# Weighted sums of the last layer: three products of rounded halves in place of one fp32 product, one step later

## What is computed

```python
S = S + jnp.eye(n, dtype=S.dtype)
h = x @ W
scores = h @ U @ h.T
mask = S > 0
scores = jnp.where(mask, scores, -jnp.inf)
att = jax.nn.softmax(scores, axis=-1)
att = att * mask.astype(att.dtype)
S_tilde = S * att
return S_tilde @ h
```

## Time and profile before

| what | us |
|---|---|
| median of three runs | 448.84 |
| the profiled execution | 449.18 |
| its span in the profile | 447.4 |
| TensorE busy (matmuls) | 404.3 |
| VectorE busy | 348.7 |
| ScalarE busy | 227.5 |
| GpSimd busy | 113.6 |

### The profile page before, as it was taken

The page is one execution under the profiler, slowest core; times in us unless marked ns, Lnnn a source line. Parts: engine busy times, 40 slices in busy tenths (PEclk is TensorE's granted clock), DMA queues, the critical chain, the costliest instruction groups (busy, mean ns, idle before and its releaser), DMA issues.

```text
span 447.4 us, 7537 instructions
## 1 busy us (share of the span) xinstructions
PE 404.3 (90%) x2596; PEld 364.4 (81%) x2596; DVE 348.7 (78%) x808; ACT 227.5 (51%) x467; POOL 113.6 (25%) x126
## 2 busy tenths in 40 slices
PE   7899999999897899999898859999599989999895
PEld 6688888999796799998898758898488778978674
DVE  5599899899875579999999956775567778768872
ACT  2243189989873778897696734214123222212230
POOL 1171000001011259431130205632000024424452
PEclk9699999999998999999999989999699999989989
DMA  8990001000000000000000000000000000010010
GB/s 259 385 370 23 1 1 49 1 0 2 0 2 1 1 1 1 3 0 2 1 0 2 1 1 0 1 1 2 1 0 1 1 1 0 0 48 1 0 48 30
DMA packets 10301, 13.96 MB, mean 31 GB/s; under 512 B 645, under 2 KB 7193, under 8 KB 10265
## 3 DMA queue, kind: packets, MB, share of 16 engines
q1 hardware_dynamic: 10264, 13.49, 8.9%
HBM read 12.10 MB, written 1.39 MB: 30 GB/s over the span
## 4 chain that ended last, share of the span: by engine, by line
PE 70%; DVE 19%; issue 7%; ACT 3%; POOL 0%; DVEq 0%; ACTq 0%
PE ps L1619 12%; PE ps L228 10%; PE ps L230 9%; PE ps L229 9%; PE ps L1355 7%; PE ps L1350 6%; PE ps L1351 6%; PE ps L1573 3%; PE ps L1574 3%; DVE s_sb L982 2%; DVE x_stats L739 2%; DVE p_lo L995 2%; PE ps L1252 2%; DVE p_lo L831 1%; DVE m_sb L817 1%
## 5 line engine op out<-in xcount | busy, mean ns | idle before, releaser
L1619 PE MATMUL ps<-v,w_ring 128*128 128x256 f32 (+3 forms) x242 | 59.1, 396 | 4.8 <-DVE x_sb L1208 3.2
L1350 PE MATMUL ps<-v_hi,p_hi 128*128 128x258 f32 (+3 forms) x242 | 63.0, 291 | 0.5 <-DVE s_sb L1036 0.4
L1351 PE MATMUL ps<-v_lo,p_hi 128*128 128x258 f32 (+3 forms) x242 | 61.1, 282 | 0.0
L1619 PEld LDWEIGHTS ps<-v,w_ring 128*128 128x128 f32 (+3 forms) x242 | 46.0, 194 | 13.4 <-issue 3.7
L228 PE MATMUL ps<-mid_hi,big_hi 128*128 128x512 f32 (+2 forms) x132 | 54.0, 409 | 2.6 <-DVE mid_lo L768 1.6
L295 POOL TENSOR_TENSOR mr_all<-mr_all,mhalf 128x4 f32<-128x4 f32 (+1 forms) x12 | 12.5, 1046 | 159.0 <-DVE mr_all L749 159.0
L391 POOL TENSOR_TENSOR total<-total,s_sb 128x512 f32<-128x512 f32 (+3 forms) x27 | 30.8, 1140 | 83.9 <-DVE w_ring L1196 83.9
L229 PE MATMUL ps<-mid_lo,big_hi 128*128 128x512 f32 (+2 forms) x132 | 49.2, 372 | 0.0
L230 PE MATMUL ps<-mid_hi,big_lo 128*128 128x512 f32 (+2 forms) x132 | 49.1, 372 | 0.0
L1350 PEld LDWEIGHTS ps<-v_hi,p_hi 128*128 128x128 f32 (+3 forms) x242 | 44.7, 185 | 2.4 <-issue 1.2
L1351 PEld LDWEIGHTS ps<-v_lo,p_hi 128*128 128x128 f32 (+3 forms) x242 | 44.7, 185 | 0.3
(11 more groups left out here) (180 smaller groups left out, 1079.5 us busy)
## 6 DMA issues: line engine op xcount, KB each, us to landing
adjT_sb<-in_adjT_dram SPq DMA_DIRECT2D x1, 2816.0 KB, 16.6
adjT_sb<-in_adjT_dram SPq DMA_DIRECT2D x3, 768.0 KB, 9.7
adjT_sb<-in_adjT_dram SPq DMA_DIRECT2D x1, 1815.0 KB, 20.9
out_dram<-x_sb SPq DMA_DIRECT2D x10, 128.0 KB
x_sb<-in_x_dram SPq DMA_DIRECT2D x2, 512.0 KB, 4.7
adjT_sb<-in_adjT_dram SPq DMA_DIRECT2D x1, 512.0 KB, 11.4
rows_sb<-in_rows_dram SPq DMA_DIRECT2D x1, 385.0 KB, 11.0
s_sb<-in_wq_dram SPq DMA_DIRECT2D x1, 256.0 KB, 4.3
```

What stands on the lines that cost most here:

```text
L1350: pe.matmul(out_ap, left_[0][0:k, n % RING, mine], right_[0][0:k, j, 0:cols_], start=(j == 0), stop=False)
L1351: pe.matmul(out_ap, left_[0][0:k, n % RING, mine], right_[1][0:k, j, 0:cols_], start=False, stop=False)
L1619: ins = pe.matmul(ps[0:rows(b), B3.sums[b % PER], 0:D], w_ring[0:k, n % RING, mine], v3[0:k, j, :], start=(j == 0), stop=(j == NB - 1))
```

## The change

- The values of the last layer go to `v_hi` as rounded halves (ScalarE), and VectorE makes their rest in the new `values3_lo(b)`, in step b (blocks 9 and 10 in step 10, block 8 in step 9). TensorE's `values(b)` now waits for that of block b - 2.
- `times_s(n)` writes an fp32 tile `full(n)` (two of them). The new `w_hi(n)` on ScalarE, behind `exp3(n + 1)`, rounds it into `p_lo`; the new `weights3_lo(n)` takes the rest into `w_lo`, on VectorE at the end of step n + 15 for even n, on GpSimd behind `add_total(n)` for odd n. `times_s(n)` waits for the rest of tile n - 2, and the copy and the rest wait for the sum of tile n - 3.
- `aggregate3` calls `weighted`: per block hi*hi and hi*lo, then, once the rest is there, lo*hi. It is a step later (LAG3 = 16), `out3` of groups 0 and 1 too (s = 11 gi + 27). `add_up` stays where it was.
- The tiles move: `total` to `raw_a` and `raw_b`, which are idle by then, and the two new weight tiles to the room of `gram`, `w3T_sb` and `u3T_sb`. `v3`, `w_ring` and the old `total` go.

```diff
--- before.py
+++ after.py
@@ -24,6 +24,7 @@
 NT = NG * NB
 CW = [min(BANK, N - g * BANK) for g in range(NG)]
 LAG = 15
+LAG3 = 16
 SLOTS = 15
 SLOTS3 = 18
 RING = 3
@@ -85,13 +86,7 @@
             p_hi, p_lo = sb("p_hi", [P, RING, BANK], F32R, early), sb("p_lo", [P, RING, BANK], F32R, early)
         more = sb("more", [P, 2 * RING, BANK])
 
-        with ExitStack() as early:
-            v_hi, v_lo = sb("v_hi", [P, NB, W], F32R, early), sb("v_lo", [P, NB, W], F32R, early)
-        with ExitStack() as late:
-            v3 = sb("v3", [P, NB, D], F32, late)
-            w_ring = sb("w_ring", [P, RING, BANK], F32, late)
-            total = sb("total", [P, 2, BANK], F32, late)
-        sb("v_home", [P, 2 * NB * W])
+        v_hi, v_lo = sb("v_hi", [P, NB, W], F32R), sb("v_lo", [P, NB, W], F32R)
 
         with ExitStack() as early:
             asa_sb = sb("asa_sb", [P, 2, D], F32, early)
@@ -102,8 +97,11 @@
         wa_hi, wa_lo = sb("wa_hi", [P, C, WA], F32R), sb("wa_lo", [P, C, WA], F32R)
         wb_hi, wb_lo = sb("wb_hi", [P, C, W], F32R), sb("wb_lo", [P, C, W], F32R)
         raw_a, raw_b = sb("raw_a", [P, C, WA]), sb("raw_b", [P, C, W])
-        gram = sb("gram", [P, C, D])
-        w3T_sb, u3T_sb = sb("w3T_sb", [P, C, D]), sb("u3T_sb", [P, C, D])
+        with ExitStack() as early:
+            gram = sb("gram", [P, C, D], F32, early)
+            w3T_sb, u3T_sb = sb("w3T_sb", [P, C, D], F32, early), sb("u3T_sb", [P, C, D], F32, early)
+        w_lo = sb("w_lo", [P, RING, BANK], F32R)
+        w_full = sb("w_full", [P, 2, BANK])
         rows_sb = sb("rows_sb", [P, 3 * D + 2])
         cols_sb = sb("cols_sb", [P, 6, C])
         ident = sb("ident", [P, P])
@@ -140,6 +138,8 @@
         def staged(k):
             return s_sb[:, k, :].rearrange("p (c n) -> p c n", c=C)
 
+        totals = [t[:, :, :].rearrange("p c n -> p (c n)")[:, 0:BANK] for t in (raw_a, raw_b)]
+
         wq_sb, wk_sb = staged(11), staged(12)
         bq_rep = s_sb[:, 14, 0:C * P].rearrange("p (c n) -> p c n", c=C)
         left = s_sb[:, 0:3, :]
@@ -157,6 +157,9 @@
 
         def sum1(n):
             return s_sb[0:rows(n % NB), 9 + n % 6, 0:CW[n // NB]]
+
+        def full(n):
+            return w_full[0:rows(n % NB), n % 2, 0:CW[n // NB]]
 
         def ring(t, n):
             return t[0:rows(n % NB), n % RING, 0:CW[n // NB]]
@@ -216,6 +219,7 @@
         rs_set, rsi_set, sal_set, joined, th_set = (sem(n) for n in ("rs_set", "rsi_set", "sal_set", "joined", "th_set"))
         p2_mm, biased, h2hi, h2lo, mask2, agg2 = (sem(n) for n in ("p2_mm", "biased", "h2hi", "h2lo", "mask2", "agg2"))
         eye_add, w_set, tot_add, tot_mm = sem("eye_add"), sem("w_set"), sem("tot_add"), sem("tot_mm")
+        vlo3, w_hi_set, w_lo_even, w_lo_odd = sem("vlo3"), sem("w_hi_set"), sem("w_lo_even"), sem("w_lo_odd")
 
 
         def wait(eng, s, value):
@@ -387,11 +391,19 @@
                 pool.wait_ge(w_set, n + 1)
                 if j:
                     wait(pool, tot_add, 10 * gi + j - 1)
-                    r = total[0:rows(j), gi % 2, 0:CW[gi]]
+                    r = totals[gi % 2][0:rows(j), 0:CW[gi]]
                     pool.tensor_tensor(r, r, slot3(n), ALU.add).then_inc(tot_add, 1)
+
+            def weights3_lo(n):
+
+                pool.wait_ge(w_hi_set, n + 1)
+                wait(pool, agg[1], n - 2)
+                pool.tensor_tensor(ring(w_lo, n), full(n), f(ring(p_lo, n)), ALU.subtract).then_inc(w_lo_odd, 1)
 
             for n in range(NT):
                 add_total(n)
+                if n % 2:
+                    weights3_lo(n)
 
 
         @block.scalar
@@ -429,8 +441,7 @@
 
                 bank = (B3 if a else B0).values[b % 2]
                 act.wait_ge(v_mm[a], b + 1)
-                dst = v3[0:rows(b), b, :] if a else v_hi[0:rows(b), b, 0:D]
-                act.activation(dst, ps[0:rows(b), bank, 0:D], ACT.Copy).then_inc(vhi[a], 1)
+                act.activation(v_hi[0:rows(b), b, 0:D], ps[0:rows(b), bank, 0:D], ACT.Copy).then_inc(vhi[a], 1)
 
             def exps(n):
 
@@ -713,11 +724,20 @@
                 act.wait_ge(s_sub[1], n + 1)
                 if j == 0:
                     wait(act, tot_mm, gi - 1)
-                    act.activation(total[0:rows(j), gi % 2, 0:CW[gi]], slot3(n), ACT.Exp, scale=-1.0 / TINY)
+                    act.activation(totals[gi % 2][0:rows(j), 0:CW[gi]], slot3(n), ACT.Exp, scale=-1.0 / TINY)
                 act.activation(slot3(n), slot3(n), ACT.Exp, scale=-1.0 / TINY).then_inc(pf[1], 1)
+
+            def w_hi(n):
+
+                act.wait_ge(w_set, n + 1)
+                wait(act, agg[1], n - 2)
+                act.activation(ring(p_lo, n), full(n), ACT.Copy).then_inc(w_hi_set, 1)
 
             for n in range(NT):
                 exp3(n)
+                if n:
+                    w_hi(n - 1)
+            w_hi(NT - 1)
 
 
         @block.vector
@@ -1192,8 +1212,20 @@
             def times_s(n):
 
                 dve.wait_ge(pf[1], n + 1)
+                wait(dve, w_lo_odd if n % 2 else w_lo_even, n // 2)
+                dve.tensor_tensor(full(n), slot3(n), adj_tile(n), ALU.mult).then_inc(w_set, 1)
+
+            def weights3_lo(n):
+
+                dve.wait_ge(w_hi_set, n + 1)
                 wait(dve, agg[1], n - 2)
-                dve.tensor_tensor(ring(w_ring, n), slot3(n), adj_tile(n), ALU.mult).then_inc(w_set, 1)
+                dve.tensor_tensor(ring(w_lo, n), full(n), f(ring(p_lo, n)), ALU.subtract).then_inc(w_lo_even, 1)
+
+            def values3_lo(b):
+
+                r, bank = rows(b), B3.values[b % 2]
+                dve.wait_ge(vhi[1], b + 1)
+                dve.tensor_tensor(v_lo[0:r, b, 0:D], ps[0:r, bank, 0:D], f(v_hi[0:r, b, 0:D]), ALU.subtract).then_inc(vlo3, 1)
 
             def out3(gi):
 
@@ -1221,15 +1253,22 @@
                     h_lo(s + 2, 3)
                 add3(s)
                 running(s, 1, ALU.min)
+                if s < 8:
+                    values3_lo(s)
+                if s == 9:
+                    values3_lo(8)
+                if s == 10:
+                    values3_lo(9)
+                    values3_lo(10)
                 if s == 3:
                     t_lo_part(1, 1)
                 if s == 9:
                     t_lo_part(2, 1)
-            for s in range(NB, NT + LAG - 1):
+            for s in range(NB, NT + LAG3 - 1):
                 for gi in range(NG):
                     if s == NB * gi + 12:
                         top(gi, 1, ALU.min)
-                    if gi < 2 and s == NB * gi + 26:
+                    if gi < 2 and s == NB * gi + 27:
                         out3(gi)
                 if s < NT:
                     add3(s)
@@ -1237,8 +1276,10 @@
                     shift(s - 13, 1)
                 if s < NT:
                     running(s, 1, ALU.min)
-                if s >= 14:
+                if 14 <= s < NT + 14:
                     times_s(s - 14)
+                if s >= 15 and (s - 15) % 2 == 0:
+                    weights3_lo(s - 15)
             out3(2)
 
 
@@ -1282,7 +1323,7 @@
                 bank = (B3 if a else B0).values[b % 2]
                 pe.wait_ge(hlo, NB * layer + b + 1)
                 if a:
-                    wait(pe, vhi[1], b - 1)
+                    wait(pe, vlo3, b - 1)
                 else:
                     wait(pe, vlo, b - 1)
                 n = D if a else W
@@ -1606,19 +1647,12 @@
 
             def aggregate3(n):
 
-                gi, j = n // NB, n % NB
-                k = rows(j)
-                pe.wait_ge(w_set, n + 1)
+                pe.wait_ge(w_hi_set, n + 1)
                 if n == 0:
-                    pe.wait_ge(vhi[1], NB)
+                    pe.wait_ge(vlo3, NB)
                     pe.wait_ge(hlo, 4 * NB)
-                if n % NB == 0:
-                    wait(pe, x_add[3], last_of(gi - 1) if gi else 0)
-                for b in blocks(gi):
-                    mine = slice((b % PER) * P, (b % PER) * P + rows(b))
-                    ins = pe.matmul(ps[0:rows(b), B3.sums[b % PER], 0:D], w_ring[0:k, n % RING, mine], v3[0:k, j, :],
-                                    start=(j == 0), stop=(j == NB - 1))
-                ins.then_inc(agg[1], 1)
+                weighted(n, B3.sums, (p_lo, w_lo), (v_hi, v_lo), D,
+                         lambda: pe.wait_ge(w_lo_odd if n % 2 else w_lo_even, n // 2 + 1), x_add[3]).then_inc(agg[1], 1)
 
             def add_up(gi):
 
@@ -1627,10 +1661,10 @@
                 for b in blocks(gi):
                     k = b % PER
                     ins = pe.matmul(ps[0:rows(b), B3.shifts[gi % 2], k:k + 1],
-                                    total[:, gi % 2, k * P:k * P + rows(b)], ones[:, :], start=True, stop=True)
+                                    totals[gi % 2][:, k * P:k * P + rows(b)], ones[:, :], start=True, stop=True)
                 ins.then_inc(tot_mm, 1)
 
-            for s in range(NT + LAG):
+            for s in range(NT + LAG3):
                 if 6 <= s <= 8:
```

(4 more changed lines are left out.)

## The result

The changed kernel takes 457.69 us (median of 4 runs, 457.07 to 458.85) where the kernel before takes 448.92 (4 runs, 448.52 to 449.75): a ratio of 1.0198, 95% interval 1.0172 to 1.0223. It is 8.8 us slower; the forecast was 458 us, 447 to 464. Its profiled execution took 458.00, with a span of 456.1. The comparisons of the experiments have their own runs of the kernel before, with medians of 449.70 to 449.82; where two experiments are set against each other, it is their ratios to these that count. An execution more than 1.5% above the fastest one of its kernel is left out of the ratios and intervals, though not of the medians.

What follows compares the result with a forecast made beforehand. TensorE bounds the kernel before; after the change VectorE and GpSimd, locking each other out, were to set the pace: 15.8 - 4.4 - 1.2 - 1.2 = +9.0 us, giving 458 us, range 447 to 464.

Steps and rivals of the forecast that it cites:

- The lock: Last layer: two-operand SBUF work of VectorE and GpSimd goes one after the other; kernel ends between 450 and 464, chance 0.68.
- TensorE's gross gain: Last layer's weighted sums: three rounded products replace a block's fp32 product, 0.36 us for 0.43; 8.8 us less for TensorE.
- The paces: Loop and tail: 3.35, 3.16, 2.75 and 1.89 us a step for 3.12, 2.64, 1.90 and 1.33; together +15.8 us.
- Values: First part of last layer: eleven values3_lo, 4.6 us, fit in VectorE's idle time; cost 0, without score-bank cover 1 to 2.
- Given back: Around both out3: with VectorE's side the bound, no half-clock loss, -4.4 us; GpSimd works off waiting operations, -1.2.
- The end: After the last times_s: a copy, a lo and three products, about 1.5 us for 2.7; -1.2 us.
- TensorE as the bound: Rival, loop and tail: the engines hardly hinder each other, TensorE still sets the pace; 441 us, chance 0.17.
- the cheapest lock: Rival, loop and tail: shorter operation times, 3.10, 2.92, 2.55, 1.71 us a step, +9.1 instead of +15.8; 451 us.
- the clock beyond 464: Rival, loop and tail: TensorE's idle gaps lower its granted clock, five us or more extra; 464 and above, chance 0.05.

Runs made afterwards that it cites:

- idle operation: The kernel before, with GpSimd also subtracting two SBUF tiles nobody reads after every odd sum, and nobody waiting for it: 449.55 us, ratio 1.0008.

## Why the prediction was right, step by step

**The lock** was the step it rested on, and it is shown: the same instruction takes 1.78 us beside a GpSimd operation and 0.68 without, a further buffer gains nothing, leaving out the sums gains 15.5 us, taking back GpSimd's low halves 8, and leaving out all low halves 17. What the experiments add: how long VectorE is held depends on the GpSimd operation, a one-input one holding it for less than half of its length; and it costs time only where VectorE or GpSimd is the bound, 0.52 us a sum in the changed kernel, 0.07 in the one before. The idle operation in the kernel before, expected at 4 to 8 us, cost nothing in the medians.

**TensorE's gross gain** of 8.8 us was right: 2.82 us a step for 3.12, 1.07 for 1.30 in the tail, and 9.1 us in all in the run without low halves, which has the change's later step and its other parts too.

**The paces.** s = 16 to 22: 20.00 us for the six steps (361.78 to 381.78), 3.33 each, forecast 3.35. With 330 columns 3.08, forecast 3.16. Tail of 512 columns 2.61 (times_s of n = 19 to that of n = 22, 418.49 to 426.32; before 1.92), forecast 2.75. Tail of 330 columns 1.75, forecast 1.89. That last one was built as three VectorE operations and then GpSimd's three, one after the other (3.78 us a pair); in fact VectorE's lie mostly beside GpSimd's, which goes round in 3.51. Over eleven steps this is 1.5 us too much.

**Values** cost nothing, as forecast: add3 of s = 13 starts at 354.57, before at 355.07, and TensorE has no wait for their rest between 320 and 356 us. VectorE idles 3.7 us before it there, for ScalarE's copies, and is not late for it at s = 13.

**Given back: wrong in its reason.** The step said that with VectorE as the bound an out3 only adds its own time and no half clock comes behind it. The windows show 0.84, 0.85 and 0.86. Those stretches did not cost what they had, presumably since TensorE was no longer the bound: from add3 of s = 22 to that of s = 27, around the first out3, it is 18.34 us, 2.9 more than five steps of 3.08; before it was 17.96, 4.8 more than five of 2.64. So 1.9 was given back where the terms, halved for one out3, had 2.8. The clock kept a price over the whole, too: the changed kernel's four executions were granted 0.957 on average, and by the line above the kernel before would take 452.0 us at that clock. Some 3 us of the loss thus go with the lower clock (an estimate; which causes which is not shown), where the forecast had put none.

**The end: wrong.** "What follows the last times_s is a copy, a lo and three products, about 1.5" became 4.7 us. It did not ask where GpSimd stands at that time, nor where the ones products stand in TensorE's order once the aggregates move. That is +3.2, of which the order, with the half clock behind it, is 1.7 (449.14 for 450.86, above); the rest is put down to GpSimd's own queue, which ends at 448.03, 1.85 us behind the last times_s.

By place: up to add3 of s = 32 the changed kernel lost 2.8 us (415.05 against 412.26; it was 0.5 ahead at s = 13), behind it 5.9 (41.05 against 35.14). The forecast's terms, with the given-back ones shared between the places, make +4.3 and +4.7. The errors cancelled, by luck; the total is better than its parts. The rivals: TensorE as the bound (441) is what the kernel would be without low halves; the cheapest lock and the clock beyond 464 did not come.

Still open: why the granted clock falls in these windows in one trace and not in another (0.84 here, 1.00 in the kernel with the idle operation). The kernel before alone ranges from 0.958 to 0.976 from execution to execution, so part of it is not the kernel's doing. No run isolates it.

## What to carry to other kernels

Before work is given to an idle engine, look in the trace for its operations beside the busy engine's: when a TENSOR_TENSOR of GpSimd met a two-SBUF-operand instruction of VectorE, they went one after the other, and 16 low halves given to GpSimd, which saved VectorE 0.6 us each, cost the kernel 8 us more than keeping them. A gain on the bound engine is had only up to the next bound, so add up the second engine's pace including such meetings (3.35 us here, against 2.7 by busy time). And when a stage is moved by one step, list everything that stands beside it in each engine's order, the small products too.

## What was not expected of the hardware

- A one-input GpSimd operation (TENSOR_SCALAR, 512 columns, fp32) held VectorE's two-operand instructions only when they began near its start: 1.02 to 1.14 us instead of 0.68, and 0.68 when begun 1.03 us behind it. The two-input one of the same size made it 1.78. The Trainium skill ("SBUF — State Buffer", Who interferes with whom) says that a VectorE instruction with two SBUF inputs contends with a GpSimd one that reads SBUF. Both kinds do here, so the trace agrees; but the one-input operation let go after an estimated 0.6 of its 1.49 us. It was the slower of the two, 1.49 us against 1.27 for an undisturbed sum of 512 columns, and took 1.80 to 1.88 us six times when it was issued under VectorE's, and 3.24 and 3.47 under several in a row.
- An operation that nobody waits for slowed its neighbour (2.64 to 2.85 us a step) and left the total where it was (449.55 against 449.82 us).
- A product of two columns with its own weights took 0.09 us on TensorE at full clock (0.37 for four, by the distance of starts), 0.07 in the tail (0.21 for three), where one with 256 columns takes 0.12. Narrow products were far from free.
